# A post-norm attention and FFN layer in float32 on one core: one written-out order per engine, and scores from Q and K with two heads in two halves of the array

## The chip, the core and the metric

The kernel runs on one core of one Trainium2 chip. TensorE multiplies matrices (PE in the rows; its weight loads are PEld), VectorE (DVE), ScalarE (ACT) and GpSimd (POOL) work on tiles, and SyncE (SP) issues the transfers. Matmuls write to PSUM, eight banks of 128 partitions x 512 float32 numbers; everything else lies in SBUF. The metric is the device time of one execution in microseconds, as the median of several.

## What is computed

The input is 32 sequences of 256 tokens with 128 features. The reference, cut to what matters:

```python
Q = (x @ Wq.T).reshape(b, n, H, R)          # H = 8 heads, R = 64
K = (x @ Wk.T).reshape(b, n, H, R)
V = (x @ Wv.T).reshape(b, n, H, d)          # d = 128
attn = softmax(einsum('bnhr,bmhr->bhnm', Q, K))
x = layernorm(x + einsum('bhnm,bmhd->bnd', attn, V))
h = silu((x @ w1.T) * s1) * ((x @ w2.T) * s2)   # 512 wide
h = gelu((h @ h1.T) * t1)
h = gelu((h @ h2.T) * t2)
x = layernorm(x + (h @ w3.T) * s3)
```

The kernel splits every float32 operand in a high part and the rest (hi, lo), and a product is three matmuls: hi x hi, hi x lo and lo x hi. The weights of the FFN are small integers here, their lo part is zero, and their products take two matmuls; a flag worked out on the chip decides that.

## The kernel before, in words

Two sequences make a pair of 512 tokens; there are 16 pairs. Scores come without Q and K: A_h = Wk_h^T Wq_h is made once per head (line 921), T_h = A_h x is a tile of 128 x 512 per head (`project_t`), and the scores of head h are T_h^T x. A pair is 16 units, one for each sequence and head. For each unit TensorE makes the scores (256 x 256, lines 769 to 771, in one of two banks `sc`), VectorE the row maxima (line 581), ScalarE the exp with its sums (432), VectorE the inverse (586), GpSimd the product with it (336), TensorE four transposes (776, two banks `pt`), ScalarE the hi part (401), VectorE the lo part (550), and TensorE times V (769 to 771 again, bank `acc`).

Loops run over steps i and, in each, over j, the 16 units of pair i. The FFN of pair i-1 is set into numbered slots of the same j loop: layer 1 in slots 5 to 8, all of layer 2 in slot 9, all of layer 3 in slot 12, layer 4 in slot 14. Layers 2 and 3 alternate with the eight V tiles and the eight T tiles of the next pair, in the program `layer23`. Scores run three units ahead (`LEAD`), times V two behind (`LAG`). Each engine executes its own list in order and waits on semaphores, so this j loop is the order of all engines. Each part of the FFN stands twice in TensorE's program, with and without the lo part of the weights, behind a branch of its own (`either`). For the last pair (`alone`) the FFN has eight banks to itself (`layer_wide`). The input is loaded in rows and turned on TensorE, four transposes a pair (`turn_x`); the weights are turned there too, in step 0.

ScalarE has one function table at a time; exp and tanh share one, gelu needs another, and the program loads it where the function changes.

Of the kernel before, what the change touches and what calls it, by code (L numbers as in the profile page):

```python
# [17 lines left out]
LEAD = 3  # L33
LAG = 2
RING = 4

AT1_SLOT = 2
NORM1_SLOTS = (0, 3)
X1T_SLOT = 4
L1_SLOTS = (5, 6, 7, 8)  # L40
L2_SLOT = 9
AT0_SLOT = 10
STATS1_SLOT = 14
L3_SLOT = 12
XT_SLOT = 14
L4_SLOT = 14
YT_SLOT = 15
NORM2_SLOT = 9

TILES_BEFORE = ((0, 1, 2), (3,), (4, 5), (6, 7))


def count(i, per, more):

    reg, off = i
    fixed = off * per + more
    return fixed if reg is None else reg * per + fixed


def plus(i, n):
    return i[0], i[1] + n


def is_first(i):
    return i[0] is None and i[1] == 0


def need(eng, sem, value):  # L70

    if not isinstance(value, int) or value > 0:
        eng.wait_ge(sem, value)


def layer_kernel(nc, x, wq, wk, wv, w1_w, w1_s, w2_w, w2_s, h1_w, h1_s, h2_w, h2_s, w3_w, w3_s, out):
    B, N, _ = x.shape
    H = wv.shape[0] // D
    R = wq.shape[0] // H
# [6 lines left out]
    V_ORDER = [(0, 0), (1, 0), (0, 1), (1, 1), (2, 0), (3, 0), (2, 1), (3, 1)]  # L86
    V_OF_UNIT = {0: 2, H // 2: 4, H: 6, H + H // 2: 8}

# [3 lines left out]
    def exists(i):  # L92

        return i[0] is not None or i[1] < PAIRS

    def row(i):
        return i[1] if i[0] is None else i[0] + i[1]

    with ExitStack() as ctx:
# [5 lines left out]


# [3 lines left out]
        NSC = 4 * KC + 2  # L110
# [3 lines left out]
        a_hi, a_lo = (sb(f"a_{s}", [P, H, D], F32R) for s in ("hi", "lo"))  # L114
# [7 lines left out]

        with ExitStack() as early:
            wq_in = sb("wq_in", [R, H, D], at=early)
            wk_in = sb("wk_in", [R, H, D], at=early)
            wv_in = sb("wv_in", [P, H, D], at=early)
# [3 lines left out]
        pt_hi, pt_lo = (sb(f"pt_{s}", [P, RING, NT, N], F32R) for s in ("hi", "lo"))  # L130
        neg_max = sb("neg_max", [P, RING, NT])
        total = sb("total", [P, RING, NT])
        inv_total = sb("inv_total", [P, RING, NT])
        x_in = sb("x_in", [P, TT, D])
# [9 lines left out]


        with ExitStack() as early:
            w1_in = sb("w1_in", [P, KC, D], at=early)
            w2_in = sb("w2_in", [P, KC, D], at=early)
            h1_in = sb("h1_in", [P, KC, HID], at=early)
            h2_in = sb("h2_in", [P, KC, HID], at=early)  # L150
            w3_in = sb("w3_in", [P, HID], at=early)
            scales_in = sb("scales_in", [NSC, P], at=early)
            lo_max = sb("lo_max", [P, 16], at=early)
            lo_flag = sb("lo_flag", [P, 4], at=early)
        x1t_hi, x1t_lo = (sb(f"x1t_{s}", [P, TOK], F32R) for s in ("hi", "lo"))
        act32 = sb("act32", [P, 2, TOK])

        odd_hi, odd_lo = (sb(f"odd_{s}", [P, KC, TOK], F32R) for s in ("hi", "lo"))
        even_hi, even_lo = (sb(f"even_{s}", [P, KC, TOK], F32R) for s in ("hi", "lo"))


        turns_buf = sb("turns_buf", [P, TOK])
        at, tanh_out, yt = turns_buf[:, 0:N], turns_buf, turns_buf


        bank = [ctx.enter_context(nc.psum_tensor(f"bank{n}", [P, 512], F32)) for n in range(8)]
        ff = bank[0:2]
        pj = bank[2]
        sc = bank[3:5]
        pt = bank[5:7]  # L170
        acc = bank[7]
        AT_BANK = [pj, ff[0]]
        X1T_BANK, YT_BANK, L4_BANK, XT_BANK = ff[1], ff[1], ff[0], pj

        T_FIRST = [pt[0], pt[1], acc, pj, ff[0], ff[1], pt[0], pt[1]]
        V_FIRST = [acc, pj, ff[0], ff[1]]

        V_BANKS = [pj, pt[(L2_SLOT + 1) % 2]]
        T_BANKS = [pj, pt[(L3_SLOT + 1) % 2]]
        PREP_BANK = [sc[0], sc[1], ff[0], ff[1]]  # L180
        SCALES_BANK, FLAG_BANK = ff[0], ff[1]


        (s_wqk, s_wv, s_wf, s_ident, s_prep_mm, s_prep_hi, s_prep_lo, s_lomax, s_flagt, s_flag,
         s_zero, s_scales_mm, s_scales, s_halves, s_held) = (sem(n) for n in (
            "wqk_in", "wv_in", "wf_in", "ident_made", "prep_mm", "prep_hi", "prep_lo", "lomax_made",
            "flag_turned", "flag_made", "zeroed", "scales_mm", "scales_ready", "halves_ready", "held"))
        s_xin, s_res, s_yfree = sem("x_in_landed"), sem("res_landed"), sem("y_stored")
        s_xt_mm, s_xt_hi, s_xt_lo = sem("xt_mm"), sem("xt_hi"), sem("xt_lo")
        s_t_mm, s_t_hi, s_t_lo = sem("t_mm"), sem("t_hi"), sem("t_lo")  # L190
# [59 lines left out]
        def units(i, j, cur, nxt, ahead):  # L250

            if j + ahead < J:
                return [(i, j + ahead)] if cur else []
# [834 lines left out]
```

## Time and profile before

| | us |
|---|---|
| median of 3 runs (1082.4 to 1082.91) | 1082.57 |
| the profiled execution | 1082.89 |
| its span on the core | 1080.6 |
| TensorE busy in the span | 1045.8 (97%) |
| TensorE's weight loads | 927.6 (86%) |
| VectorE busy | 818.3 (76%) |
| ScalarE busy | 816.2 (76%) |
| GpSimd busy | 603.4 (56%) |

Some groups of instructions of that execution, mean ns of one:

| engine, what | shape | mean ns |
|---|---|---|
| ScalarE exp, and the read of its sum | 128 x 256 | 473, 203 |
| ScalarE copy of a turned unit, hi part | 128 x 512 | 599 |
| ScalarE tanh, gelu | 128 x 512 | 691, 690 |
| VectorE row maxima | 128 x 512 | 678 |
| VectorE lo part of a turned unit | 128 x 512 | 674 |
| VectorE normalisation of x1 in a steady pair | 128 x 128 | 730 |
| GpSimd product with the inverse | 128 x 512 | 1042 |
| GpSimd lo part | 128 x 512 | 1296 |

Rows give start and duration in us. The end of a matmul is modelled and lies behind the start of the next one, so the distance between starts is what a matmul takes of TensorE. A weight load lies on a row of its own. "Issue" behind a row is time in which the engine waited for nothing that the profile shows.

### The profile page before, as it was taken

The numbers are of one execution on the slowest core, as the hardware profiler recorded it, in microseconds if no ns is written. First come the engines' busy times: TensorE is split into PE (matmuls) and PEld (weight loads), VectorE is DVE, ScalarE is ACT, GpSimd is POOL, SyncE is SP. The second block draws the span as 40 slices with busy tenths as digits, with TensorE's granted clock in tenths as the row PEclk, the third lists the DMA queues.
The fourth block names the chain that finished last, engine by engine and source line by source line (L and its number), as shares of the span: only waits on it lengthen the run. The fifth ranks groups of instructions, "written<-read, shape, count | busy, mean of one in ns | idle before, by whom it ended". The sixth has DMA issues, their size and how long they took to land.

```text
span 1080.6 us, 19355 instructions
## 1 busy us (share of the span) xinstructions
PE 1045.8 (97%) x6598; PEld 927.6 (86%) x6598; DVE 818.3 (76%) x1722; ACT 816.2 (76%) x1948; POOL 603.4 (56%) x603
## 2 busy tenths in 40 slices
PE   7998999999999999999999999999999999999976
PEld 6878898888989889898888989888898988989864
DVE  5889687686968869687786968768687786968654
ACT  5768778787877878788787877878787787878732
POOL 1316457456565656657466665745656565655743
PEclk9999999999999999999999999999999999999988
DMA  6000000000000000000000000000000000000000
GB/s 175 12 10 12 1 21 2 20 12 11 21 12 17 6 21 12 11 21 5 18 12 20 12 12 21 1 21 12 12 21 11 11 11 11 12 11 12 10 2 19
DMA packets 29850, 18.12 MB, mean 17 GB/s; under 512 B 914, under 2 KB 28580, under 8 KB 29732
## 3 DMA queue, kind: packets, MB, share of 16 engines
q1 hardware_dynamic: 29732, 16.53, 5.3%
q8 instruction: 76, 1.25, 0.5%
q14 instruction: 42, 0.34, 0.1%
HBM read 12.33 MB, written 4.19 MB: 15 GB/s over the span
## 4 chain that ended last, share of the span: by engine, by line
PE 67%; DVE 15%; issue 7%; ACT 6%; POOL 5%; DMA 0%; SPq 0%; ACTq 0%; POOLq 0%; DVEq 0%
PE bank L850 13%; PE bank L851 13%; PE bank L769 11%; PE bank L771 11%; PE bank L770 11%; PE bank L776 7%; DVE neg_max L581 4%; DVE x L623 4%; POOL prob L336 3%; DVE pt_lo L550 3%; ACT prob L432 2%; ACT L432 2%; POOL rstd L353 1%; ACT pt_hi L401 1%; DVE t_lo L550 1%
## 5 line engine op out<-in xcount | busy, mean ns | idle before, releaser
L336 POOL TENSOR_TENSOR prob<-prob,inv_total 128x512 f32<-128x512 f32 x256 | 266.6, 1042 | 199.8 <-DVE inv_total L586 198.3
L432 ACT ACTIVATE prob<-bank,neg_max 128x256 f32<-128x256 f32 x512 | 238.1, 473 | 74.9 <-DVE neg_max L581 74.4
L343 POOL TENSOR_TENSOR odd_lo<-act,odd_hi 128x512 fp32r<-128x512 f32 x120 | 155.5, 1296 | 169.1 <-DVE odd_hi L648 116.7
L550 DVE TENSOR_TENSOR pt_lo<-bank,pt_hi 128x512 fp32r<-128x512 f32 x256 | 172.5, 674 | 58.8 <-ACT pt_hi L401 58.7
L581 DVE TENSOR_REDUCE neg_max<-bank 128x2 f32<-128x512 f32 x256 | 173.4, 678 | 0.1
L769 PE MATMUL bank<-pt_hi,v_hi 128*128 128x256 f32 x512 | 164.9, 322 | 0.0
L401 ACT ACTIVATE pt_hi<-bank 128x512 fp32r<-128x512 f32 x256 | 149.8, 599 | 10.2 <-PE bank L776 8.2
L776 PE MATMUL bank<-ident,prob 128*128 128x128 f32 x1024 | 154.0, 273 | 1.7 <-issue 0.7
L769 PE MATMUL bank<-xt_hi,t_hi 128*128 128x256 f32 x512 | 150.2, 293 | 5.1 <-ACT prob L432 3.9
L771 PE MATMUL bank<-xt_hi,t_lo 128*128 128x256 f32 x512 | 144.3, 282 | 0.0
L771 PE MATMUL bank<-pt_hi,v_lo 128*128 128x256 f32 x512 | 144.0, 281 | 0.0
L770 PE MATMUL bank<-xt_lo,t_hi 128*128 128x256 f32 x512 | 143.9, 281 | 0.0
L770 PE MATMUL bank<-pt_lo,v_hi 128*128 128x256 f32 x512 | 143.9, 281 | 0.0
L550 DVE TENSOR_TENSOR t_lo<-bank,t_hi 128x512 fp32r<-128x512 f32 x128 | 87.8, 688 | 45.8 <-ACT t_hi L401 44.9
L776 PEld LDWEIGHTS bank<-ident,prob 128*128 128x128 f32 x1024 | 116.7, 140 | 4.6 <-issue 2.2
L343 POOL TENSOR_TENSOR even_lo<-act,even_hi 128x512 fp32r<-128x512 f32 x60 | 77.5, 1291 | 68.5 <-DVE even_hi L648 66.0
L550 DVE TENSOR_TENSOR v_lo<-bank,v_hi 128x512 fp32r<-128x512 f32 x128 | 87.2, 684 | 32.6 <-ACT v_hi L401 31.7
L401 ACT ACTIVATE v_hi<-bank 128x512 fp32r<-128x512 f32 x128 | 77.0, 603 | 44.3 <-PE bank L771 43.8
L401 ACT ACTIVATE t_hi<-bank 128x512 fp32r<-128x512 f32 x128 | 76.8, 600 | 43.3 <-PE bank L771 41.9
L769 PEld LDWEIGHTS bank<-xt_hi,t_hi 128*128 128x128 f32 x512 | 96.4, 188 | 14.1 <-issue 7.7
L432 ACT ACTIVATION_READ_ACCUMULATOR prob<-bank,neg_max 128x1 f32 x512 | 103.8, 203 | 0.0
L459 ACT ACTIVATE act<-bank,scales 128x512 f32<-128x512 f32 x120 | 82.6, 690 | 25.1 <-PE bank L851 22.7
(116 smaller groups left out, 2564.7 us busy)
## 6 DMA issues: line engine op xcount, KB each, us to landing
x_in<-in_L_attn_x SPq DMA_DIRECT2D x16, 256.0 KB, 2.8
res<-in_L_attn_x SPq DMA_DIRECT2D x16, 256.0 KB, 2.8
out_x<-y SPq DMA_DIRECT2D x16, 256.0 KB, 2.3
h_in<-in_L_ffn_h_w SPq DMA_DIRECT2D x2, 1024.0 KB
w_in<-in_L_ffn_w_w SPq DMA_DIRECT2D x3, 256.0 KB
wv_in<-in_L_attn_Wv SPq DMA_DIRECT2D x1, 512.0 KB, 6.3
wq_in<-in_L_attn_Wq SPq DMA_DIRECT2D x1, 256.0 KB, 4.4
wk_in<-in_L_attn_Wk SPq DMA_DIRECT2D x1, 256.0 KB, 5.3
```

What stands on the lines that cost most here:

```text
L336: nc.gpsimd.tensor_tensor(prob[:, j % RING, :, :], prob[:, j % RING, :, :], inv_total[:, j % RING, :].unsqueeze(2).to_broadcast([P, NT, N] ...
L343: nc.gpsimd.tensor_tensor(lo[:, c, :], act_of(f, c), hi[:, c, :].bitcast(F32), ALU.subtract).then_inc(s_lo, 1)
L401: return nc.scalar.activation(dst, src, ACT.Copy)
L432: last = nc.scalar.activation(prob[:, j % RING, nt, :], sc[j % 2][:, nt * N:(nt + 1) * N], ACT.Exp, bias=neg_max[:, j % RING, nt:nt + 1], ...
L550: return nc.vector.tensor_tensor(dst, src, hi.bitcast(F32), ALU.subtract)
L581: nc.vector.tensor_reduce(neg_max[:, j % RING, :], sc[j % 2].rearrange("p (t m) -> p t m", m=N), AX.X, ALU.max, negate=True).then_inc(s_ma ...
L769: mm(dst, w_hi, m_hi, start=start, stop=False)
L770: mm(dst, w_hi, m_lo, start=False, stop=False)
L771: return mm(dst, w_lo, m_hi, start=False, stop=stop)
L776: last = turn(dst[:, n * P:(n + 1) * P], b, ident[:, :])
L850: mm(dst, w_hi[c], m_hi[c], start=(c == 0), stop=False)
L851: last = mm(dst, w_hi[c], m_lo[c], start=False, stop=(c == n - 1 and not with_lo))
```

## The change

- **Scores.** Q and K are projected, four tiles of 128 x 512 each with two heads on the upper and lower 64 partitions (`query_or_key`); `scores(i, g)` makes two heads at once, their matmuls alternating between rows 0 to 63 and 64 to 127 of the array and between banks 5 and 6. There is no T and no A_h.
- **Inputs.** The host hands over x once more in turned layout, and all weights turned; the transposes of x and of the weights on TensorE are gone. ScalarE and VectorE split the attention weights, GpSimd the FFN's.
- **Order.** The slots, loops over j and the rules that set them are gone. One cycle k is written out per engine as a list of calls, and run for k = 0 to 18. It spreads the QKV tiles of the next pair and half layers of the FFN over all 16 units. The last pair uses the same lists; `alone` is gone.
- **Banks.** A table names one PSUM bank for each tile: 3 for all turned probabilities, 2 and 4 for Q, K, V and the attention's output, 0 and 1 for the FFN, 5 and 6 for the scores, 7 for times V.
- **Branch.** One branch in TensorE's program, at the end of cycle 0, with all later cycles in two versions.
- **Work moved.** Four of the FFN's twelve lo parts and the last normalisation go from GpSimd to VectorE.

```diff
+T_BANK = (2, 2, 4, 4, 2, 4, 2, 2)
+V_BANK = (4, 2, 4, 4, 2, 4, 2, 4)
+TURN_BANK = (3, 3, 3, 3, 3, 3, 3, 3, 3, 3, 3, 3, 3, 3, 3, 3)
...
+            def scores(i, g):
+
+                if there(i):
+                    b, t = 2 * g // H, 2 * g % H
+                    if b == 0:
+                        pe.wait_ge(s_t_lo, after(i, H, t + 2))
+                    need(pe, s_exp, after(i, J, 2 * g))
                     m = slice(b * N, (b + 1) * N)
-                    last = three(sc[j % 2][:, nt * N:(nt + 1) * N], t_hi[:, h, q], t_lo[:, h, q],
-                                 hi[:, m], lo[:, m], True, True)
...
-                    mm(dst, w_hi[c], m_hi[c], start=(c == 0), stop=False)
-                    last = mm(dst, w_hi[c], m_lo[c], start=False, stop=(c == n - 1 and not with_lo))
+                    for nt in range(NT):
+                        q = slice(b * N + nt * P, b * N + (nt + 1) * P)
+                        ends = []
+                        for term, (left, right) in enumerate(((t_hi, t_hi), (t_hi, t_lo), (t_lo, t_hi))):
+                            for n in range(2):
+                                rows = slice(n * R, (n + 1) * R)
+                                ends.append(mm(sc[n][:, nt * N:(nt + 1) * N], left[rows, t, q], right[rows, t + 1, m],
+                                               start=(term == 0), stop=(term == 2)))
+                    ends[-2].then_inc(s_sc, 1)
+                    ends[-1].then_inc(s_sc, 1)
...
+                t_high(k + 1, 1)
+                acc_copy(k, 0)
+                gelu2(k - 1, 0)
+                t_high(k + 1, 2)
+                pt_high(k, 10)
+                gelu2(k - 1, 1)
+                exp(k, 14)
+                exp(k, 15)
+                v_high(k + 1, 1)
+                pt_high(k, 11)
+                gelu2(k - 1, 2)
...
+                t_low(k + 1, 5)
+                high(k - 1, 3, 1)
+                xt_low(k + 2)
+                norm2(k - 2)
+                low(k - 1, 3, 1)
...
+            with pe.If(any_lo):
+                for k in range(1, PAIRS + 3):
```

What the lists become in the order of the instructions:

TensorE, a steady pair, around one block of scores. Before: the scores of one unit (xt is the input, t is T), four transposes, and times V, all with 128 rows.

```order
L769 MATMUL bank<-xt_hi,t_hi 128x256
L770 MATMUL bank<-xt_lo,t_hi 128x256
L771 MATMUL bank<-xt_hi,t_lo 128x256
L769 MATMUL bank<-xt_hi,t_hi 128x256
L770 MATMUL bank<-xt_lo,t_hi 128x256
L771 MATMUL bank<-xt_hi,t_lo 128x256
L776 MATMUL bank<-ident,prob 128x128 x4
L769 MATMUL bank<-pt_hi,v_hi 128x256
L770 MATMUL bank<-pt_lo,v_hi 128x256
L771 MATMUL bank<-pt_hi,v_lo 128x256
L769 MATMUL bank<-pt_hi,v_hi 128x256
L770 MATMUL bank<-pt_lo,v_hi 128x256
```

After: a tile of Q, two heads' scores (t is the tile of Q and K; in each "x2" one matmul has rows 0 to 63 and bank 5, the other rows 64 to 127 and bank 6), and a half layer.

```order
L846 MATMUL bank<-xt_hi,wq_hi 128x512
L847 MATMUL bank<-xt_lo,wq_hi 128x512
L848 MATMUL bank<-xt_hi,wq_lo 128x512
L891 MATMUL bank<-t_hi 128x256 x2
L891 MATMUL bank<-t_lo,t_hi 128x256 x2
L891 MATMUL bank<-t_hi,t_lo 128x256 x2
L891 MATMUL bank<-t_hi 128x256 x2
L891 MATMUL bank<-t_lo,t_hi 128x256 x2
L891 MATMUL bank<-t_hi,t_lo 128x256 x2
L958 MATMUL bank<-even_hi,h_hi 128x512
L959 MATMUL bank<-even_lo,h_hi 128x512
L961 MATMUL bank<-even_hi,h_lo 128x512
```

The scores stand in eight blocks of twelve a pair where sixteen of six stood; in front of and behind each block is work with 128 rows.

ScalarE, layer 2 of a steady pair. Before: one change to gelu, four gelus with the copies of V between them, and one change back.

```order
L459 ACT_TABLE_LOAD [waits l1_lo]
L459 ACTIVATE act<-bank,scales 128x512 [waits l2_mm]
L401 ACTIVATE v_hi<-bank 128x512 [waits v_mm]
L459 ACTIVATE act<-bank,scales 128x512 [waits l1_lo,l2_mm]
L401 ACTIVATE v_hi<-bank 128x512 [waits v_mm] x2
L459 ACTIVATE act<-bank,scales 128x512 [waits l2_lo,l2_mm]
L401 ACTIVATE v_hi<-bank 128x512 [waits v_mm] x2
L459 ACTIVATE act<-bank,scales 128x512 [waits l2_lo,l2_mm]
L432 ACT_TABLE_LOAD [waits pt_mm]
L432 ACTIVATE prob,total<-bank,neg_max 128x256 [waits max]
```

After: the same four gelus in two groups of two, with the exps of two units between.

```order
L199 ACTIVATE t_hi<-bank 128x512 [waits scores,t_mm]
L199 ACTIVATE at<-bank 128x256 [waits at_mm,pv]
L432 ACT_TABLE_LOAD [waits l3_lo2]
L432 ACTIVATE gelus<-bank,scales 128x512 [waits l2_mm]
L199 ACTIVATE t_hi<-bank 128x512 [waits scores,t_mm]
L199 ACTIVATE pt_hi<-bank 128x512 [waits pv,pt_mm]
L432 ACTIVATE gelus<-bank,scales 128x512 [waits l3_lo3,l2_mm]
L383 ACT_TABLE_LOAD [waits pt_mm]
L383 ACTIVATE prob,total<-bank,neg_max 128x256 [waits max]
L383 ACTIVATE prob,total<-bank,neg_max 128x256
L383 ACTIVATE prob,total<-bank,neg_max 128x256 [waits pt_mm,max]
L383 ACTIVATE prob,total<-bank,neg_max 128x256
```

What moved is the second pair of gelus, behind the exps; layer 3 is dealt out in the same way.

GpSimd, layer 2 and the last normalisation. Before:

```order
L343 TENSOR_TENSOR even_lo<-act,even_hi 128x512 [waits l2_hi]
L351 TENSOR_SCALAR var_eps<-mv 128x4 [waits mv2]
L353 TENSOR_TENSOR rstd<-var_eps,minus_half 128x4 [waits var_eps2]
L343 TENSOR_TENSOR even_lo<-act,even_hi 128x512 [waits rstd2,l2_hi]
L357 TENSOR_SCALAR y<-y,mv,rstd 128x128
L343 TENSOR_TENSOR even_lo<-act,even_hi 128x512 [waits l2_hi]
L357 TENSOR_SCALAR y<-y,mv,rstd 128x128
L343 TENSOR_TENSOR even_lo<-act,even_hi 128x512 [waits l2_hi]
L336 TENSOR_TENSOR prob<-prob,inv_total 128x512 [waits inv]
```

After (rstd is still made there, the normalisation of y and the fourth lo part of the layer are not):

```order
L196 TENSOR_TENSOR even_lo<-gelus,even_hi 128x512 [waits l2_hi0]
L196 TENSOR_TENSOR even_lo<-gelus,even_hi 128x512 [waits l2_hi1]
L248 TENSOR_TENSOR prob<-prob,inv_total 128x512 [waits inv]
L196 TENSOR_TENSOR even_lo<-gelus,even_hi 128x512 [waits l2_hi2]
L248 TENSOR_TENSOR prob<-prob,inv_total 128x512 [waits inv]
L281 TENSOR_SCALAR var_eps<-mv 128x4 [waits mv2]
L283 TENSOR_TENSOR rstd<-var_eps,minus_half 128x4 [waits var_eps2]
L248 TENSOR_TENSOR prob<-prob,inv_total 128x512 [waits inv]
```

Both went to VectorE's list.

## Rows read from the trace of the kernel before

**Rows 1.** The stretches: us, busy us of each engine (instructions), clock, DMA share, GB/s

```profile
24.00:78.70 54.70, 49.63 (x349) 43.68 (x346) 47.23 (x94) 39.68 (x113) 16.61 (x16) 1.00 0.04 10
...
336.30:400.60 64.30, 64.13 (x410) 57.29 (x409) 49.84 (x106) 50.95 (x123) 38.49 (x39) 1.00 0.05 14
979.00:1038.60 59.60, 57.96 (x386) 51.94 (x384) 44.83 (x100) 42.48 (x106) 39.43 (x40) 1.00 0.04 10
1038.60:1080.60 42.00, 26.34 (x98) 18.56 (x98) 21.20 (x54) 11.66 (x19) 12.91 (x14) 0.82 0.05 13
```

**Rows 2.** The chain of waits in order of time: start us, us, what

```profile
138.83 1.28 ACT L432
...
910.33 1.28 ACT L432
```

**Rows 3.** The timeline at the second layer: start us, us, engine, line, operation

```profile
500.77 0.40 PE L851 MATMUL bank<-odd_lo,h_hi 128*128 128x512 f32 x1
500.78 0.19 PEld L850 LDWEIGHTS bank<-odd_hi,h_hi 128*128 128x128 f32 x1
501.01 0.40 PE L850 MATMUL bank<-odd_hi,h_hi 128*128 128x512 f32 x1
```

**Rows 4.** The timeline of TensorE at scores, four transposes and times V

```profile
505.08 0.28 PE L769 MATMUL bank<-xt_hi,t_hi 128*128 128x256 f32 x1
...
505.32 0.28 PE L771 MATMUL bank<-xt_hi,t_lo 128*128 128x256 f32 x1
505.44 0.61 PE L776 MATMUL bank<-ident,prob 128*128 128x128 f32 x4
...
506.00 0.28 PE L770 MATMUL bank<-pt_lo,v_hi 128*128 128x256 f32 x1
```

**Rows 5.** The timeline of the weight loads, behind a gap

```profile
345.25 0.19 PEld L769 LDWEIGHTS bank<-xt_hi,t_hi 128*128 128x128 f32 x1 [0.27 <-issue]
345.36 0.19 PEld L770 LDWEIGHTS bank<-xt_lo,t_hi 128*128 128x128 f32 x1
```

**Rows 6.** The timeline from 128 rows to 18 and back

```profile
31.67 0.60 PE L776 MATMUL bank<-ident,x_in 128*128 128x128 f32 x4
...
32.20 0.13 PEld L961 LDWEIGHTS bank<-ident,scales_in 18*128 18x128 f32 x1 [0.17 <-issue]
32.20 0.23 PE L961 MATMUL bank<-ident,scales_in 18*128 18x18 f32 x1
...
32.36 0.19 PEld L769 LDWEIGHTS bank<-xt_hi,t_hi 128*128 128x128 f32 x1
...
32.58 0.28 PE L770 MATMUL bank<-xt_lo,t_hi 128*128 128x256 f32 x1
```

**Rows 7.** The timeline of TensorE at the start

```profile
7.28 3.78 PE L921 MATMUL bank<-wk_in,wq_in 64*128 64x128 f32 x16 [1.94 <-DMA wk_in<-in_L_attn_Wk]
...
12.61 0.77 PE L769 MATMUL bank<-xt_hi,a_hi 128*128 128x512 f32 x1
```

**Rows 8.** The tile that is loaded next: ns min/median/max, first to last start

```profile
L776 PEld LDWEIGHTS bank<-ident,wv_in x8: 183/226/229, 11.0 to 12.3; 128*128 128x128 f32 x8
...
L296 SPq DMA_DIRECT2D wv_in<-in_L_attn_Wv x1: 624/624/624, 2.6 to 2.6; - x1
...
DMA to landing us min/median/max: 6.3/6.3/6.3
```

**Rows 9.** ScalarE's groups in one pair: busy us, mean ns of one

```profile
L459 ACT ACT_TABLE_LOAD x2 | 2.6, 1283 | 0.0
```

**Rows 10.** VectorE's groups in the tail, same columns

```profile
L550 DVE TENSOR_TENSOR even_lo<-prob,even_hi 128x512 fp32r<-128x512 f32 x4 | 2.9, 718 | 0.1
...
L614 DVE TENSOR_SCALAR y<-y,mv,rstd 128x128 f32<-128x128 f32 x4 | 1.1, 344 | 1.7 <-POOL rstd L353 1.7
```

**Rows 11.** The chain of waits in the tail

```profile
1045.25 0.79 PE bank L850
...
1050.86 0.49 PE bank L900
```

More of the change, by code:

```diff
@@ new lines, in x1t_low, with silu @@
+            def x1t_low(f):
+                if there(f):
+                    dve.wait_ge(s_x1t_hi, f + 1)
+                    minus(nc.vector, x1t_lo[:, :], bank[X1T_BANK][:, :], x1t_hi[:, :]).then_inc(s_x1t_lo, 1)
+            def silu(f, c):
+                if there(f):
+                    dve.wait_ge(s_tanh, after(f, KC, c + 1))
+                    need(dve, s_1lo[(c + 2) % KC], f if c < 2 else f + 1)
+                    nc.vector.scalar_tensor_tensor(out=gated[:, c % 2, :], in0=tanh_out[:, :], scalar=1.0,
+                                                   in1=bank[Z1_BANK[c]][:, :], op0=ALU.add,
+                                                   op1=ALU.mult).then_inc(s_silu, 1)
@@ new lines, in low, with y_add @@
+            def low(f, layer, c):
+                if there(f):
+                    full, hi, lo, _, s_hi, s_lo = LAYER[layer]
+                    dve.wait_ge(s_hi[c], f + 1)
+                    minus(nc.vector, lo[:, c, :], full[:, c % 2, :], hi[:, c, :]).then_inc(s_lo[c], 1)
+            def y_add(f):
+                if there(f):
+                    dve.wait_ge(s_yt_mm, f + 1)
+                    need(dve, s_yfree, 16 * f)
+                    nc.vector.tensor_tensor(y[:, :, :], bank[YT_BANK].rearrange("p (t d) -> p t d", d=D),
+                                            x1[:, :, :], ALU.add).then_inc(s_yadd, 1)
@@ L764, in _, with free @@
             mm, turn = nc.tensor.matmul, nc.tensor.transpose
-            any_lo = []
+            def free(*readers):
+                for s, i, per, n in readers:
+                    need(pe, s, after(i, per, n))
             def three(dst, w_hi, w_lo, m_hi, m_lo, start, stop):
@@ new lines, in turn_attention, with turn_x1 @@
+            def turn_attention(i, b, *readers):
+                if there(i):
+                    pe.wait_ge(s_acc, after(i, 2, b + 1))
+                    free(*readers)
+                    turns(bank[AT_BANK[b]], [at[:, t * P:(t + 1) * P] for t in range(NT)], s_at)
+            def turn_x1(f, *readers):
+                if there(f):
+                    pe.wait_ge(s_x1, after(f, 2, 2))
+                    free(*readers)
+                    turns(bank[X1T_BANK], [x1[:, t, :] for t in range(TT)], s_x1t_mm)
@@ new lines, in turn_y, with turn_flag @@
+            def turn_y(f, *readers):
+                if there(f):
+                    pe.wait_ge(s_yt, f + 1)
+                    free(*readers)
+                    turns(bank[YT_BANK], [yt[:, t * P:(t + 1) * P] for t in range(TT)], s_yt_mm)
+            def turn_flag(k):
+                if k == 0:
+                    pe.wait_ge(s_lomax, NWF + 1)
+                    pe.wait_ge(s_wf_lo, NWF)
+                    turn(FLAG_BANK[0:1, 0:P], lo_max[:, 15:16], ident[:, :]).then_inc(s_flagt, 1)
@@ L1072 @@
+            scores(0, 2)
+            values(0, 3, (s_t_lo, 0, H, 7))
+            pe.wait_ge(s_ident, 1)
+            cycle(0, False)
+            pe.wait_ge(s_flag, 1)
+            any_lo = pe.value_load(lo_flag[0:1, 0:1].bitcast(I32))
+            with pe.If(any_lo):
+                for k in range(1, PAIRS + 3):
+                    cycle(k, True)
+            with pe.Else():
+                for k in range(1, PAIRS + 3):
+                    cycle(k, False)
 def kernel(**inputs):
```

1554 lines of the change are left out of this document (795 added, 759 removed).

## The prediction

> **What bounds the kernel now.** I read the stretches first. In one period of the steady part TensorE is busy 64.13 of 64.30 us, ScalarE 50.95, VectorE 49.84 and GpSimd 38.49, at full clock [rows 1]. One piece of the chain of waits, ScalarE's change of function table before an exp, returns at 138.83 and, twelve pairs later, at 910.33 [rows 2]: 771.5 / 12 = 64.29 us for a pair. A busy share can hide gaps, since matmuls overlap, so I take the distance from start to start [rows 3, 4]: a matmul of 512 columns follows the one before by 0.233 us, one of 256 columns by 0.12 (505.08 to 505.32 for two; over longer runs 0.1185), and four transposes plus the refill behind them take 0.44, 0.11 each (505.44 to the matmul whose successor starts at 506.00, so 505.88).
>
> A pair has, by the code, 136 matmuls of 512 columns (24 T, 24 V, 16 in layer 1, 32 + 32 + 8 in layers 2 to 4), 192 of 256 columns (96 scores, 96 times V) and 80 transposes: 136 x 0.233 + 192 x 0.1185 + 80 x 0.11 = 31.7 + 22.8 + 8.8 = 63.3 us. Waits are the missing 1.0. So TensorE's own work is the bound, and whatever leaves TensorE shortens the pair until ScalarE or VectorE stands in the way.
>
> **The change part by part.**
>
> *Work of TensorE that stays.* Q and K take the place of T with as many matmuls (8 tiles of three), and V, the layers and times V are the same. 31.7 + 96 x 0.1185 = 43.1 us.
>
> *Turned inputs.* Four transposes of x a pair go: 80 to 76, -0.44 us.
>
> *Scores.* Per pair there are still 96 matmuls of 256 columns, but each uses 64 rows, and two heads alternate between the upper and lower half of the array and between two banks. The trace has nothing like it, so three things are bounded.
> First, the streams. If the two halves run side by side, 48 steps of 0.1185 are left: 5.7 us for 11.4. If they don't, 11.4.
> Second, the weight loads. Behind a gap, with nothing to hide under, one load starts at 345.25 and the next at 345.36 [rows 5]: the loader is taken for 0.11 us, nearly all of the 0.1185 that a 256-column matmul leaves. If the halves stream together but loads go one by one, a step of two costs 2 x 0.108 = 0.216, and 48 steps 10.4 us: the gain shrinks to 1.0.
> Third, the change of shape. Where the program goes from 128 rows to 18 and back, the load doesn't slip under the running matmuls as elsewhere: it starts at 32.20, 0.07 before the modelled end of the transposes (31.67 + 0.60), and the next one at 32.36, 0.07 before the end of the small one [rows 6]. The array is drained each time. From 32.11, where the four transposes would be through, to 32.46, where the first score starts (0.12 before 32.58), two changes cost 0.32 us, 0.16 each. With 64 rows at the start it looks the same: sixteen pieces run from 7.28 for 3.78 us [rows 7], and the next load starts only at 11.0, where they are all but through, although its data, asked for at 2.6, landed 6.3 later [rows 8]. Between matmuls of 256 columns it is 0.28 - 0.07 + 0.11 - 0.12 = 0.20. There are 8 blocks of scores, each between 128-row work, so 16 changes: 2.6 to 3.2 us, and I take 3.2.
>
> What the halves do beside each other no row tells. The 64-row matmuls at the start all use the same half. I take the side-by-side case for loads and streams, because the halves share neither partitions nor bank, and keep both others as cases. The scores are then 5.7 + 3.2 = 8.9 us for 11.4: -2.5.
>
> The Trainium skill, "TensorEngine Tiling (Array Packing)", section Key Properties, says that changing the tiling mode drains TensorE, and that tiles load and multiply in parallel; for the first, rows 6 agree. Its section Theoretical Speedup gives up to 2x for 64 rows; taken alone, without drains, that would make the scores 5.7 us. The page "TensorE: Matmul & The Clock Gate", section Measured speedup vs the span model, says that loads overlap with matmuls in flight only where the row groups differ; here the trace differs, as on one and the same full array the load at 500.78 starts with the matmul at 500.77 [rows 3].
>
> TensorE's pair: 64.3 - 0.44 - 2.5 = 61.4 us, the old 1.0 of waits still in it.
>
> *ScalarE.* A pair has now two loads of the gelu table and two of the exp table, 1.283 us each [rows 9]. The new order deals the gelus out in four groups of two with exps between them: four and four. +4 x 1.283 = 5.1 us. The rest is the same count. 50.95 + 5.1 = 56.1 of 61.4. It waits 13.3 us a pair now and may wait 5.3 then.
>
> *VectorE.* Four low parts come over from GpSimd, 0.72 each where VectorE did them in the tail, and the last normalisation, four pieces of 0.34 alone to 0.73 beside a busy GpSimd [rows 10]: +2.9 + 1.4 to 2.9. 49.84 becomes 54.1 to 55.6. GpSimd falls by as many ops.
>
> *One bank for all turned probabilities, fixed banks elsewhere.* A transposed tile must be copied by ScalarE (0.60) and subtracted by VectorE (0.67) before the next may be turned; with TensorE's 0.44 that is some 1.9 us a unit, 30 a pair: no bound on average. But between turns 4 and 7 TensorE has only 1.7 to 2.0 us of other work, and around gelu group one ScalarE has two tables (2.6), two gelus (1.4), two exps (1.8), three copies and more, 9.2 us against TensorE's 7.7 of turns 9 to 11. TensorE will wait there, and behind its wait stand the layers and the next projections. Lower bound 0, upper bound 2 us a pair; I take 0.6. Old waits may also vanish (the gap before 345.25), so the lower end of the sum is below 61.4 by up to 1.
>
> *Branches.* Seven per pair become one in the program. They were hidden, as TensorE was fed all the time: 0. At the end of cycle 0 TensorE now waits for the flag and the jump with nothing queued: +1 to +3, once.
>
> *Start.* First matmul of a projection at 12.61 now [rows 7], behind the product of Wq and Wk and eight transposes. After, it needs the arrived weights (7.3) and two splits on ScalarE and VectorE (0.6, 0.6, 0.7): 9.2, -3.4. The first unit is turned at 24.0 and step 0 lasts 54.7 [rows 1]. In the new cycle 0 GpSimd splits eleven weight tiles, each a copy (about 1.0 to 1.3) and a subtraction (1.3) beside a 1.04 normalisation, some 3.5 us a unit for eleven units, and the other five units at 2.5 to 3: about 51. With the jump: -3.4 - 3.7 + 2, and half of the first is eaten by four more tiles ahead of cycle 0: I take -3 (0 to -8).
>
> *Last softmax step.* 59.6 us now [rows 1]. It loses 11 tiles and three blocks of scores instead of 8 tiles and three units, and is bound by chains: -3 (0 to -6).
>
> *Tail.* 42.0 us now [rows 1]. The old code gives the last pair eight banks: layer 1 begins at 1045.25 and layer 2 at 1050.86 [rows 11]. The new order is the same everywhere, so each chunk waits for the half-gated one before: z (two matmuls and 0.17 until it is readable, 0.64), tanh (0.69 and 0.06 for the signal), silu (the same) is 2.15 a chunk; the fourth has z2 and gate behind it and is split 10.7 us after the start. Half of layer 2 runs meanwhile: +2 (0 to +5).
>
> *Sum.* A pair: 61.4 + 0.6 = 62.0, -2.3. The execution took 1082.9 (span 1080.6 and 2.3 around it), the median 1082.6. 1082.9 - 14 x 2.3 - 3 - 3 + 2 = 1046.7; against the median 1046.4. I say 1047.
>
> **Rivals.**
> *A, the forecast*: both halves at once, drains of 0.2, small waits. 61.4 to 62.8 a pair, 1035 to 1062.
> *B, loads go one by one* (the slower side). Place: the 12 matmuls of each block. Price 10.4 + 3.2 = 13.6 for 11.4, +2.2, less 0.44: 66.0 a pair. 1082.9 + 14 x 1.75 - 4 = 1103. It decides from where a step of two costs more than (11.4 + 0.44 - 3.2) / 48 = 0.18 us. For it: the 0.11 us that a load holds the loader, and that nothing in the trace shows two loads at once. Against it: the halves have separate partitions.
> *C, nothing overlaps*: the change doesn't do what it says. 11.4 + 3.2: 67.1 a pair, 1118.
> *D, drains are much cheaper than in rows 6* or hide: the scores 5.7 to 6.5, TensorE 58.5 to 59; then ScalarE with 56.1 and its waits sets about 59.5 to 60.5: 1012 to 1027. The skill's up to 2x, named above, is this case.
> *E, the halves work, but the in-order engines don't keep up*: ScalarE at 56 and VectorE at 55, single banks; 63 to 64.5 a pair, 1061 to 1082. For it: all three engines over 88% busy. Against: before, TensorE hardly waited for either.
>
> **How the numbers follow.** A 0.47, D 0.14, E 0.11, B 0.20, C 0.08. The likeliest is A: 1047. Eight in ten: leaving out C and the lower part of D, 1018 to 1108; A's own range is 1035 to 1062. About 0.2% (2.2 us) is what a measurement can tell from no change. Faster: A, D and two thirds of E, 0.68; same 0.04; slower: B, C and the end of E, 0.28.
>
> **What would show it.** The period, from the returning table load. In the timeline of a block of scores: pairs of matmuls 0.12 apart (A, D), 0.22 (B) or 0.24 (C), and the gap "issue" before the first load of each block and behind it (0.2, or none for D). In the lines: eight table loads a pair, ScalarE near 56 and VectorE near 55 busy. Under A TensorE's waits for ScalarE and VectorE are under 1.6 us a pair, under E over 2. What would make me wrong: loads one by one, or an order whose waits add up though each engine has room.

## The result, and the profile after

| | before | after |
|---|---|---|
| median | 1082.54 us (1082.40 to 1082.91) | 1030.74 us (1029.68 to 1031.28) |
| the profiled execution, its span | 1082.89, 1080.6 | 1031.28, 1029.4 |

The ratio is 0.952, with a 95% interval of 0.9503 to 0.9536. The forecast was 1047 with a range of 1018 to 1108, so the time lies inside the range and on the side it named, 16 us below. It lies outside the 1035 to 1062 that the prediction gave its likeliest case, A. The same kernel timed again later gave 1030.73 us (ratio 0.9511).

The head of the page, busy time and share of each engine:

```profile
PE 984.3 (96%) x6465; PEld 816.5 (79%) x6465; DVE 827.1 (80%) x1827; ACT 859.1 (83%) x1992; POOL 513.0 (50%) x509
```

It answers to the table of before. A steady pair after, as [rows 1], is the first stretch here; the other lies in layer 1 of the last pair:

```profile
444.88:505.04 60.16, 60.16 (x407) 50.50 (x406) 50.87 (x114) 54.33 (x125) 30.85 (x31) 1.00 0.05 14
...
990.00:1000.00 10.00, 7.13 (x15) 3.57 (x14) 4.91 (x7) 4.23 (x7) 3.00 (x3) 0.50 0.00 0
```

TensorE is busy all 60.16 us of a pair. To see a pair's length I take one piece of the chain of waits, a block of scores, at two places nine pairs apart:

```profile
204.25 0.91 PE bank L891 x12
...
745.68 0.91 PE bank L891 x12
```

541.43 / 9 = 60.16 us, before 64.29. To split the rest, three rows of TensorE's timeline, where the first unit of pair 0, of pair 1 and of pair 15 is turned. Before:

```profile
23.97 0.38 PE L776 MATMUL bank<-ident,prob 128*128 128x128 f32 x2
...
79.55 0.38 PE L776 MATMUL bank<-ident,prob 128*128 128x128 f32 x2
...
982.74 0.38 PE L776 MATMUL bank<-ident,prob 128*128 128x128 f32 x2
```

and after:

```profile
27.83 0.38 PE L852 MATMUL bank<-ident,prob 128*128 128x128 f32 x2
...
82.23 0.45 PE L852 MATMUL bank<-ident,prob 128*128 128x128 f32 x1 [4.72 <-issue]
...
927.00 0.44 PE L852 MATMUL bank<-ident,prob 128*128 128x128 f32 x2
```

| stretch | before | after | difference | predicted |
|---|---|---|---|---|
| up to pair 1 | 79.55 | 82.23 | +2.7 | -3 |
| 14 pairs | 903.19 | 844.77 | -58.4 | -32.2 |
| from pair 15 to the end of the span | 97.9 | 102.4 | +4.5 | -1 |

(The last two predicted values are 14 x -2.3, and the last softmax step's -3 with the tail's +2. The first is the start's -3, the jump included.) The pairs gave 26 us more than forecast, and the two ends took 11 of that back.

A block of scores after, TensorE's matmuls and, from the same stretch, its weight loads:

```profile
504.65 0.40 PE L959 MATMUL bank<-even_lo,h_hi 128*128 128x512 f32 x1
504.97 0.39 PE L891 MATMUL bank<-t_hi 64*128 64x256 f32 x2
505.19 0.28 PE L891 MATMUL bank<-t_lo,t_hi 64*128 64x256 f32 x2
...
505.67 0.28 PE L891 MATMUL bank<-t_hi,t_lo 64*128 64x256 f32 x2
505.88 0.66 PE L852 MATMUL bank<-ident,prob 128*128 128x128 f32 x4
```

```profile
504.97 0.19 PEld L891 LDWEIGHTS bank<-t_hi 64*128 64x128 f32 x2 [0.36 <-issue]
505.08 0.19 PEld L891 LDWEIGHTS bank<-t_lo,t_hi 64*128 64x128 f32 x2
```

"x2" is one matmul for each head. The pairs follow at 0.12, as a single matmul of 128 rows did in [rows 4]. The 512-column matmul ahead is followed after 0.32 us and not 0.23, the first pair after 0.22 and not 0.12, the last pair after 0.21.

### The profile page after: what moved, and what is told of

The parts are those of the page before. It is cut to its first block, busy times and chain, and to the rows that moved or that the text cites. A ratio compares the mean times of both kernels' runs of the same rounds, so it can differ in the third digit from the quotient of the medians.

```text
span 1029.4 us, 19535 instructions
## 1 busy us (share of the span) xinstructions
PE 984.3 (96%) x6465; PEld 816.5 (79%) x6465; DVE 827.1 (80%) x1827; ACT 859.1 (83%) x1992; POOL 513.0 (50%) x509
## 4 chain that ended last, share of the span: by engine, by line
PE 91%; DVE 4%; ACT 2%; issue 2%; DMA 0%; POOLq 0%; SPq 0%; DVEq 0%; POOL 0%; ACTq 0%
PE bank L852 13%; PE bank L958 13%; PE bank L959 13%; PE bank L846 12%; PE bank L848 11%; PE bank L847 11%; PE bank L891 11%; PE bank L938 3%; PE bank L939 3%; ACT prob L383 1%; DVE pt_lo L196 1%; DMA wk_in<-in_wk_t 0%; DVE neg_max L600 0%; DVE t_lo L196 0%; DVE v_lo L196 0%
## 5 line engine op out<-in xcount | busy, mean ns | idle before, releaser
L846 PE MATMUL bank<-pt_hi,v_hi 128*128 128x256 f32 x512 | 151.9, 297 | 0.0
L196 POOL TENSOR_TENSOR even_lo<-gelus,even_hi 128x512 fp32r<-128x512 f32 x48 | 61.8, 1288 | 103.7 <-DVE even_hi L678 103.7
L383 ACT ACTIVATION_READ_ACCUMULATOR prob<-bank,neg_max 128x1 f32 x512 | 108.3, 212 | 0.0
L958 PE MATMUL bank<-odd_hi,h_hi 128*128 128x512 f32 x256 | 107.0, 418 | 0.0
L958 PE MATMUL bank<-even_hi,h_hi 128*128 128x512 f32 x256 | 105.6, 412 | 0.2 <-DVE even_lo L196 0.2
L847 PEld LDWEIGHTS bank<-pt_lo,v_hi 128*128 128x128 f32 x512 | 98.3, 192 | 4.3
L959 PE MATMUL bank<-odd_lo,h_hi 128*128 128x512 f32 x256 | 101.5, 397 | 0.0
L846 PEld LDWEIGHTS bank<-pt_hi,v_hi 128*128 128x128 f32 x512 | 98.1, 192 | 4.0
L959 PE MATMUL bank<-even_lo,h_hi 128*128 128x512 f32 x256 | 101.1, 395 | 0.0
L848 PEld LDWEIGHTS bank<-pt_hi,v_lo 128*128 128x128 f32 x512 | 98.3, 192 | 0.0
```

What stands on the lines that cost most here:

```text
L196: return eng.tensor_tensor(dst, src, hi.bitcast(F32), ALU.subtract)
L383: last = nc.scalar.activation(prob[:, slot(i, u, RING), nt, :], sc[u % 2][:, nt * N:(nt + 1) * N], ACT.Exp, bias=neg_max[:, u, nt:nt + 1], ...
L846: mm(dst, w_hi, m_hi, start=start, stop=False)
L847: mm(dst, w_hi, m_lo, start=False, stop=False)
L848: return mm(dst, w_lo, m_hi, start=False, stop=stop)
L958: mm(dst, w_hi[:, c, cols], m_hi[:, c, :], start=begins, stop=False)
```

## The experiments

Each is the changed kernel with the edit shown. Its period is taken as above.

**Is it the two halves?** Three kernels change only which matmul stands where, or on which rows.

```diff
-                        for term, (left, right) in enumerate(((t_hi, t_hi), (t_hi, t_lo), (t_lo, t_hi))):
-                            for n in range(2):
+                        for n in range(2):
+                            for term, (left, right) in enumerate(((t_hi, t_hi), (t_hi, t_lo), (t_lo, t_hi))):
```

> The changed kernel with one edit: in each block the six matmuls of the first head (rows 0 to 63, bank 5) are issued and then the six of the second (rows 64 to 127, bank 6), no longer in turns. Theory (the score saving comes from two row halves that load and stream side by side, and TensorE takes its matmuls in order): without turns each matmul of 256 columns takes its 0.118 us alone, a block of 12 takes 1.42 us for 0.71, a pair 8 x 0.71 = 5.7 us more: period 65.9 us for 60.16, total about 1031 + 14 x 5.7 + 5 = 1116, slower than the kernel before the change. Rival (TensorE overlaps matmuls of different halves also when they are not next to each other, or the gain is not from the overlap but from the shorter 64-row matmuls): period near 60.2 to 62, total 1031 to 1056.

Measured: 1032.07 us (ratio to before 0.9529, 0.9513 to 0.9545), 1.3 us above after; the period is 60.21 for 60.16. The text on record misdescribes the edit: it stands inside the loop over the halves of the queries, so the program has three matmuls of one head, three of the other, and again. Still, if each had to start behind the one ahead of it in the program, only neighbours at the seams could run together: nine steps for six, half of the price, 2.8 us a pair. In TensorE's timeline they run together:

```profile
503.81 0.39 PE L891 MATMUL bank<-t_hi 64*128 64x256 f32 x2
504.03 0.29 PE L891 MATMUL bank<-t_lo,t_hi 64*128 64x256 f32 x2
```

Both heads start at 503.81 and go on in pairs, as in after, although the partner stands three matmuls later in the program. My theory was wrong in one premise, that TensorE starts its matmuls strictly in program order. That left two questions: how far ahead it looks, and whether the gain comes from the overlap at all.

```diff
-                    for nt in range(NT):
-                        ...
-                            for n in range(2):
+                    for n in range(2):
+                        rows = slice(n * R, (n + 1) * R)
+                        for nt in range(NT):
```

> The changed kernel with one edit: in each block of scores all six matmuls of the first head (rows 0 to 63, bank 5) are issued, then all six of the second (rows 64 to 127, bank 6). The run before this one (e1) was described as that, but its edit sat inside the loop over the halves of the queries: it issued runs of three, and still ran two streams side by side 0.01 us apart. Theory now (each half of the rows takes its own matmuls from a queue, and TensorE's sequencer runs ahead of a busy half): if at least six fit, the period stays at 60.2, total 1030 to 1033. Rival (only about three fit, or the overlap reaches only that far): part of each block is alone, up to 3 steps of 0.118 in a block, 8 blocks: +0.9 to +2.8 us a pair, total 1045 to 1075.

Measured: 1072.47 us (0.9909, 0.9894 to 0.9924), the rival's upper end. TensorE's timeline of one block:

```profile
504.18 0.38 PE L890 MATMUL bank<-t_hi 64*128 64x256 f32 x1
504.40 0.28 PE L890 MATMUL bank<-t_lo,t_hi 64*128 64x256 f32 x1
504.52 0.28 PE L890 MATMUL bank<-t_hi,t_lo 64*128 64x256 f32 x1
504.52 0.39 PE L890 MATMUL bank<-t_hi 64*128 64x256 f32 x2
504.75 0.28 PE L890 MATMUL bank<-t_lo,t_hi 64*128 64x256 f32 x2
504.86 0.28 PE L890 MATMUL bank<-t_hi,t_lo 64*128 64x256 f32 x2
504.98 0.28 PE L890 MATMUL bank<-t_hi 64*128 64x256 f32 x1
```

The second head's first matmul starts at 504.52, beside the first head's third (the "x2" row of 504.52 is this one and the first head's fourth). So it starts ahead of three matmuls of the first head that stand before it in the program, and no earlier. Its own last three run alone. It is some 0.35 us behind the first head, three steps: nine steps for six, 8 x 3 x 0.118 = 2.8 us a pair; the period is 62.89, 2.73 more. So TensorE reaches past about three waiting matmuls of a busy half. That a queue of this length holds them is my reading; the reach is what the two runs show, for matmuls of 256 columns.

```diff
-                                rows = slice(n * R, (n + 1) * R)
+                                rows = slice(0, R)
```

> The changed kernel with both heads of a block read from rows 0 to 63 (the computation is changed: the odd heads' scores are those of the even heads); order, banks, shapes and count are the same, only the second half of the array is never used. Theory (the saving of the scores comes from the two halves at work together): each matmul of 256 columns takes its 0.118 alone, a block 1.42 for 0.71 us, a pair 5.7 more: period 65.9, total 1031 + 14 x 5.7 + 5 = 1116. Rival (matmuls with 64 rows are themselves twice as fast, the halves do nothing for each other): period 60.2.

Measured: 1119.67 us (1.0332, 1.0317 to 1.0348), 3% slower than before the change, and a period of 65.81 (busy row below), 5.65 more than after; 5.7 was expected. A pair of matmuls now takes 0.24:

```profile
485.41 0.39 PE L891 MATMUL bank<-t_lo,t_hi 64*128 64x256 f32 x2
485.65 0.40 PE L891 MATMUL bank<-t_hi,t_lo 64*128 64x256 f32 x2
```

```profile
420.87:486.68 65.81, 65.81 (x405) 56.17 (x404) 51.01 (x114) 54.73 (x126) 30.86 (x30) 1.00 0.04 13
```

This is the prediction's case C, built as a kernel (67.1 there, with the old waits in it). The overlap of the halves is the whole gain of the scores: without it the rest of the change doesn't pay for the drains.

**What does a change of shape cost?** Seven blocks are cut in half with another operation between:

```diff
-                scores(k, 3)
+                scores(k, 3, (0,))
                 ...
+                scores(k, 3, (1,))
```

> The changed kernel with one edit: seven of the eight blocks of scores in a pair are cut in half, with one tile or half layer that was behind the block now between the halves. Same matmuls, but the array goes from 128 to 64 rows and back 15 times a pair and not 8: 14 more changes. Theory (each change drains the array for about 0.2 us, as the trace of after shows around the blocks): 14 x 0.2 = 2.8 us a pair, period 63.0 for 60.16, total about 1031 + 15 x 2.8 = 1073. Rival (the drains are hidden or are a fixed part of something else): period 60.2 to 60.6, total under 1037.

Measured: 1078.37 us (0.9958, 0.9942 to 0.9975). The same matmuls in a period of 63.20, 3.04 more for 14 more changes, so 0.217 us each at most. A half block in TensorE's timeline shows where it lies:

```profile
518.46 0.40 PE L848 MATMUL bank<-xt_hi,wq_lo 128*128 128x512 f32 x1
518.79 0.39 PE L892 MATMUL bank<-t_hi 64*128 64x256 f32 x2
519.01 0.28 PE L892 MATMUL bank<-t_lo,t_hi 64*128 64x256 f32 x2
519.13 0.28 PE L892 MATMUL bank<-t_hi,t_lo 64*128 64x256 f32 x2
519.34 0.50 PE L960 MATMUL bank<-even_hi,h_hi 128*128 128x512 f32 x1
519.67 0.40 PE L961 MATMUL bank<-even_lo,h_hi 128*128 128x512 f32 x1
```

On each side of the change one distance is 0.1 too long: the one into the new shape (0.33 for 0.23, then 0.21 for 0.12), and the one behind its first matmul (0.22 for 0.12, then 0.33 for 0.23). The four make 0.38 for the way in and out, 0.19 a change, or 2.7 us for 14. The rest is no drain: twice in this pair TensorE waits for data, 0.2 us each.

```profile
478.03 0.87 DVE x L645 x3
```

```profile
478.62 0.28 PE L848 MATMUL bank<-pt_hi,v_lo 128*128 128x256 f32 x1
478.94 0.66 PE L852 MATMUL bank<-ident,x 128*128 128x128 f32 x4
```

Here the transposes of x start 0.32 and not 0.12 behind the matmul ahead, when VectorE is through with x; at 480.29 four others start 0.42 behind a pair of scores and not 0.21. (3.04 - 0.41) / 14 is 0.19 again. My reading is that the array runs empty, and that the first load has nothing to hide under, so that the second waits; the distances are measured, this cause of theirs is not shown. The Trainium skill, "TensorEngine Tiling (Array Packing)", section Key Properties, says that a change of mode drains TensorE and that tiles load and multiply in parallel. The traces agree with both; the price, 0.19 us here, and the reach of three matmuls it doesn't give.

**Does ScalarE stand close behind?**

```diff
-                    nc.scalar.activation(gelus[:, o % 2, :], bank[L2_BANK[o]][:, :], ACT.Gelu,
+                    nc.scalar.activation(gelus[:, o % 2, :], bank[L2_BANK[o]][:, :], ACT.Tanh,
```

> The changed kernel with tanh in place of the gelus of layers 2 and 3 (that part of the computation is another one): ScalarE then never changes its function table, and eight loads of 1.28 us a pair, 10.3 us, go. Theory (TensorE's own work sets the period, ScalarE with 54 of 60 busy is hidden): the period stays at 60.1 to 60.2; only the end, where ScalarE's chain is bare, and the first cycles lose table loads, 2 to 6 us: total 1025 to 1029. Rival (ScalarE sets the period or is level with TensorE): the period falls by 0.5 us or more, total under 1020.

Measured: 1028.47 us (0.95, 0.9484 to 0.9516). A period of that kernel:

```profile
443.11:503.27 60.16, 60.16 (x406) 50.50 (x404) 50.42 (x113) 44.29 (x117) 30.86 (x30) 1.00 0.05 14
```

ScalarE has 10 us less to do and the period doesn't move by 0.01. The eight table loads are fully hidden in a steady pair; the 2.3 us by which the run is shorter lie outside of these pairs.

**The end of cycle 0.** In the chain of waits of after:

```profile
77.63 0.29 DVE lo_flag L570
77.92 4.31 issue
82.23 1.09 PE bank L852 x4
83.32 0.43 PE bank L846
...
84.17 1.37 issue
```

The flag is ready at 77.9, and the next matmul starts at 82.2, at half the clock (0.43 for a 512-column matmul). The trace has TensorE reading the flag at 77.95 for 0.49 us and then one compare-and-branch at 78.50 of 3.57 us. A second stretch of 1.37 us in which TensorE waits for nothing that the profile shows follows two matmuls later. Two kernels ask about it, one without the branch and one with the two versions in the other order in the program:

```diff
-            pe.wait_ge(s_flag, 1)
-            any_lo = pe.value_load(lo_flag[0:1, 0:1].bitcast(I32))
-            with pe.If(any_lo):
-                ...
-            with pe.Else():
-                ...
+            for k in range(1, PAIRS + 3):
+                cycle(k, False)
```

> The changed kernel without the flag and the branch behind cycle 0: TensorE goes straight on in the version without the lo part of the FFN's weights (the other version is left out). Theory (the chain of waits shows 4.31 and 1.37 us of issue there, and the clock granted is 0.55 in the stretch behind it): 5 to 8 us once, period unchanged at 60.16, total 1023 to 1026. Rival (the gap there is only where VectorE and GpSimd, late in cycle 0, would have held TensorE anyway): under 1.5 us.

Measured: 1021.66 us (0.9431, 0.9415 to 0.9447), 9.1 less than after and more than I expected. The gap itself is some 5 us. The rest lies behind it: in 80 to 90 us the granted clock is 1.00 in this kernel and 0.55 in after, and the cycle behind it is 57.7 us long for 62.7.

```diff
-            with pe.If(any_lo):
+            with pe.If(any_lo < 1):
                 for k in range(1, PAIRS + 3):
-                    cycle(k, True)
+                    cycle(k, False)
             with pe.Else():
                 for k in range(1, PAIRS + 3):
-                    cycle(k, False)
+                    cycle(k, True)
```

> The changed kernel with one edit: the two versions of the later cycles change places in the program, so that the one that runs (without the lo part) stands right behind the branch and the other one is jumped to. Theory (the trace of after puts 3.57 us on the one compare-and-branch at 78.5, where the program jumps over 18 cycles of code, and 0.21 on each of the old kernel's 112 short jumps): without the far jump the branch takes about 0.2 us; 3.4 us go directly, and a part of the slow stretch behind it, 4 to 9 us in all, total 1022 to 1027. Rival (the time is that of reading the flag and of a cold start behind any branch): within 1.5 us of 1030.7.

Measured: 1024.13 us (0.9446, 0.9429 to 0.9462), 6.6 less than after. Its chain of waits:

```profile
77.44 0.29 DVE lo_flag L570
77.73 0.84 issue
78.57 0.94 PE bank L852 x4
```

0.84 for 4.31, and the second stretch, of 1.37, is gone: it was the far jump, not the flag. The flag is read for 0.49 us as before, and the compare-and-branch behind it, at 78.31, takes 0.09. The jump over the other version now stands at the end of the program: 3.28 us at 1015.2, where TensorE has nothing left but its last four transposes. What this run still has above the one without a branch is 2.5 us; it has the 0.84 and a clock that stays at half until about 82.1 (91.2 in after). The old kernel's 112 short branches, with TensorE fed, took 0.21 us each (median, in TensorE's queue). The Trainium skill, "Advanced Engine Details and Errata", section Control Flow Timing, gives about 108 ns for a compare-and-branch; here the trace has 0.09 where the program goes straight on, and differs where it jumps, 0.21 for a short jump and 3.57 for the far one.

**The tail and the start.** Layer 1 of the last pair, in the chain of after, from its first matmul to the next chunk's, and its end:

```profile
988.68 0.67 PE bank L938
989.35 0.44 PE bank L939
989.82 0.70 ACT tanh_out L414
990.54 0.70 DVE gated L658
...
991.28 0.80 PE bank L938
...
1000.09 0.43 PE bank L958
```

That is 11.4 us to layer 2 for 5.6 before [rows 11], with each chunk behind the tanh and the silu of the one before, and the clock falls to half (990 to 1000, the second stretch above).

```diff
+        def z1_bank(f, c):
+            return bank[(0, 2, 5, 3)[c] if f == LAST else Z1_BANK[c]]
```

(and likewise for z2 and layers 2 and 3, whose waits for a bank fall away in the last pair)

> The changed kernel with one edit: the FFN of the last pair, with nothing beside it, has eight banks to itself, as in the kernel before, so that TensorE runs ahead of tanh and silu. Theory (the tail grew because layer 1 waits for each chunk's chain: 11.4 us from layer 1 to layer 2, before 5.6, and the clock fell to half there): 4 to 6 us less, total 1025 to 1027. Rival (the chain through ScalarE and VectorE of the fourth chunk is as long whatever TensorE does): under 1.5 us less.

Measured: 1023.59 us (0.9457, 0.9438 to 0.9476), 7.1 less. Its profiled execution was 2.2 us above its own median, and shows 98.7 us from pair 15 on for 102.4, so 3.7; another 1.2 lie ahead of pair 1, where nothing was edited. The other runs narrow it: from pair 15 to the end the four profiles with these banks (this one and the three below that build on it) take 97.9 to 98.7 us, and four without them (after, the same again, no branch, the version that falls through) 102.4 to 103.5. The means are 4.8 apart, inside the 4 to 6 expected; the other 2.3 of the 7.1 stay open.

```diff
+            t_high(0, 4)
+            t_high(0, 5)
+            t_high(0, 6)
             exp(0, 2)
             exp(0, 3)
             v_high(0, 0)
-            t_high(0, 4)
-            t_high(0, 5)
-            t_high(0, 6)
```

(with VectorE's list likewise)

> The last pair's banks as in the run beside it and, in the start, the hi and lo parts of the first pair's Q and K tiles 4 to 6 split ahead of the exps 2 and 3, not behind them. Theory (TensorE waits 2.9 us for a split at 23.2 and has its clock lowered in 20 to 40 us): another 2 to 4 us, total 1021 to 1024. Rival (the start is bound by something else, such as the row maxima and exps that are now later): within 1 us of the run with the banks alone, or slower.

Measured: 1020.39 us (0.9419, 0.9407 to 0.9432), 3.2 less than with the banks alone. The first unit is turned at 24.56, for 26.55 and, in after, 27.83; in the two runs below with the same start it is 22.7 and 24.2.

```diff
-            cycle(0, False)
+            cycle_a(0, False)
+            cycle_b(0, False)
+            cycle_a(1, False)
             pe.wait_ge(s_flag, 1)
```

> The version with the last pair's banks and the earlier splits in the start, and besides the wait for the flag and the branch moved from the end of cycle 0 to a quarter into cycle 1, just ahead of the first layer that needs the flag; the flag has long been ready there. Theory (without the branch the kernel was 9.1 us shorter; the old code's branches, placed among queued matmuls with the flag ready, showed no gap): 4 to 9 us less than the same version with the early branch (1020.4), total 1011 to 1016. Rival (reading the flag and fetching the instructions behind the jump stall TensorE wherever it stands): within 2 us of 1020.4.

Measured: 1017.20 us (0.9396, 0.9383 to 0.9409): 3.2 less, under the 4 to 9 expected. The far jump is in TensorE's timeline there too, with the flag long ready:

```profile
84.22 0.28 PE L862 MATMUL bank<-pt_hi,v_lo 128*128 128x256 f32 x1
87.12 0.79 PE L952 MATMUL bank<-x1t_hi,w_hi 128*128 128x512 f32 x1 [2.61 <-issue]
```

Its branch starts at 83.61 and takes 3.45 us; the queued matmuls cover it up to 84.34 (84.22 and the 0.12 that one takes), some 0.7 us, no more.

> Last pair's banks, earlier splits in the start, the branch a quarter into cycle 1, and the version that runs standing right behind it. Theory (all four add up; 2.6 us of issue and a clock lowered behind the far jump are what the version with the later branch, 1017.2, still has): 3 to 5 us less, total 1012 to 1014. Rival (the jump is no matter): 1017.

Measured: 1012.63 us (0.9347, 0.9334 to 0.9359), 4.6 less than the run before it, and 18.1 less than after. It is the fastest version here; its period is the same 60.16.

> The changed kernel once more, with nothing edited, on the chip and in the rounds of a new comparison. The version with the last pair's banks was 7.1 us shorter than it in the medians, but its trace shows only 3.7 us less behind the last pair and 1.3 us less ahead of the first turned unit, where nothing was edited. If that is spread of the start from one loading to the next, this run may be 1 to 3 us off 1030.7 and its first turned unit between 26 and 28.5; if the banks really bring 7, it repeats 1030.7 within 0.5.

Measured: 1030.73 us (0.9511, 0.9498 to 0.9524), the first one's time to 0.01. The first unit is turned at 27.23 here. Between the kernels with the same start that point lies at 26.3 to 28.5 us (31.3 with the scores on one half), so in one profile a difference of a microsecond or two at the start is spread.

## Why the prediction was right, and where its sum was off

- **Bound.** TensorE's own work sets the period before and after; the run without table loads settles it for after. Right.
- **Scores.** 48 steps of 0.118 and 16 changes: 5.7 + 3.2 = 8.9 us forecast; 5.7 + 16 x 0.19 = 8.7 by the rows. Case A's mechanism holds for loads and streams, and the run on one half shows it by its absence. B falls with the pair of loads that start together; the first row of loads above holds both at 504.97. The drain taken from [rows 6], 0.2, was 0.19. (What the prediction takes from the Trainium skill's page "TensorE: Matmul & The Clock Gate" on loads and row groups stands there in the section The mechanism.)
- **Waits: the step that failed.** 61.4 kept the old 1.0 us of waits, and 0.6 of new ones were added to make 62.0. Without both, the same terms are 31.7 + 11.4 + 8.4 + 5.7 + 3.2 = 60.4, and with 0.19 for a change 60.2; the period is 60.16, so no wait is left at all. The 4.1 us by which a pair is shorter are then 2.7 of scores, 0.4 of turned inputs and 1.0 of waits. 1.84 us too much by 14 pairs is 26 us. From the chain of waits of before I could have seen that the old 1.0 belonged to the order that was being replaced: in one pair it leaves TensorE for GpSimd and VectorE, as in the rows 468.09 and 470.18 below; after, the chain of a steady pair names TensorE alone. Which part of the change took the waits away no run here tells, since none has the new scores in the old order. For the single bank for turned probabilities I took 0.6 of 0 to 2 us, and 0 was right. Over the pair the engines had 5.8 us (ScalarE) and 9.3 (VectorE) left; why the one stretch of ScalarE's list that was longer than TensorE's work beside it (9.2 us against 7.7 by the prediction) held nothing up is not taken apart.
- **ScalarE, VectorE.** Forecast 56.1, and 54.1 to 55.6; measured 54.33 and 50.87. There are eight table loads a pair, as said. VectorE came out lighter in part because two of its operations got shorter: the normalisation of x1 takes 0.34 for 0.73, the hi part in even_hi 0.59 for 0.76, together 2.3 us a pair. The 0.73 is a mean of two kinds. Before, two of the four pieces a pair take 0.33 and two 1.06 to 1.19: the one at 470.18 takes 1.06, with GpSimd's product beside it from 470.11 to 471.15. After, the pieces of x1 don't fall together with the start of such a product, but of the four of y at 501.56 three take 0.34 and the last 1.06, with GpSimd's product from 502.20 to 503.31.

```profile
468.09 1.04 POOL prob L336
...
470.18 1.06 DVE x L623
```

```profile
L645 DVE TENSOR_SCALAR x<-res,mv,rstd 128x128 f32<-128x128 f32 x4 | 1.1, 342 | 0.1
...
L678 DVE CAST even_hi<-gelus 128x512 fp32r<-128x512 f32 x4 | 2.3, 586 | 0.2 <-ACT gelus L432 0.2
```

- **Branch.** +1 to +3 forecast; 9.1 measured by leaving it out. The step priced a wait and a jump, not a jump over 18 cycles of code, and not the clock that it costs.
- **Start.** The first projection starts at 8.79 (9.2 forecast). But I set four more tiles against half of that gain. TensorE reaches the first turned unit 19.0 us later, where before it was 11.4 (12.61 to 23.97), with two waits of 1.6 and 2.9 us for an exp and a split, and a clock of 0.83 and 0.66 in 20 to 40 us. -3 became +2.7 up to pair 1, branch included.
- **Last step and tail.** -3 and +2 forecast, +4.5 together measured. Parted at the first matmul of layer 1 (988.68, before 1045.25), the last softmax step gave 0.8 us and not 3, and the tail took 5.4 more and not 2, above its own 0 to 5. The chain of 2.15 us a chunk was named, and measured 2.6 to 2.7, since TensorE's part of it runs at half the clock there (0.43 for a 512-column matmul): that was not in the sum.
- **Rivals.** The period, 60.16, lies in D's 59.5 to 60.5 and not in A's 61.4 to 62.8, and the time lies between D's 1012 to 1027 and A's 1035 to 1062. But D's reasons did not come: the drains cost what A says, and ScalarE does not set the period. It is A's mechanism without A's waits. E never came: nothing of the order's waits reaches TensorE.
- **Luck.** With the 14 pairs as measured and the ends as forecast the time would have been 1082.9 - 58.4 - 4 = 1020.5, 26 below the forecast. That it is 16 is luck: the ends were wrong the other way.

## What to carry to other kernels

When an order is replaced, its waits can go with it, as all of them did here: build the sum from the work of the engine that sets the pace, and add waits only as a bound. Two heads in two halves of the array give their factor of two only while the partner stands within three matmuls, and each pair of changes takes 0.38 us back, so a block must be long: here 12 matmuls save 0.71 and pay 0.38. What runs once (a far jump, a first split, a last layer with single banks) costs twice, itself and the half clock behind it; here three such places together held 18 us of 1031.

## What the runs showed of the hardware that I had not expected

- TensorE starts a matmul on an idle half ahead of up to three earlier ones on the busy half.
- A change between 128-row and 64-row matmuls costs 0.19 us, by the rows above half of it ahead of the first matmul and half behind it.
- A compare-and-branch of TensorE takes 0.09 us when the program goes straight on, 0.21 when it jumps to code near by, and 3.45 to 3.57 when it jumps over 18 cycles of code; laid out so that the version that runs follows the branch, the gap is 0.84, flag and all.
- VectorE's 128 x 128 normalisation takes 0.33 to 0.35 us or, where a 128 x 512 product of GpSimd starts between 0.13 us before it and 0.07 after it, 1.06 to 1.19: it ends 0.08 us behind that product (471.24 for 471.15, 503.39 for 503.31). Of the steady pairs before and after only one piece, of 0.45 at 817.43, is neither.
